# Loading a run's weight addresses into TensorE's registers one half-step earlier, from padded rows, in a macaron block of two mixture-of-experts layers and an RWKV attention

## What is computed

```python
x = x + 0.5 * ffn(ln(x))          # mixture of experts, top 2 of 8
x = x + attention(ln(x))          # RWKV: token shift, k, v, r, wkv recurrence over 512 tokens, Wo
x = x + 0.5 * ffn(ln(x))          # the same experts again

def ffn(x):
    probs = softmax(x @ gate_w)                       # (8*512, 8)
    weights, indices = top_k(probs, 2); weights /= weights.sum(-1)
    for i in range(8):                                # w1, w3: 128x512, w2: 512x128
        wi = where(indices == i, weights, 0).sum(-1)
        out += ((silu(x @ w1[i]) * (x @ w3[i])) @ w2[i]) * wi
```

## Time and profile before

| | us |
|---|---|
| median of 3 executions | 621.75 |
| lowest, highest | 621.48, 623.04 |
| the profiled execution | 623.24 |
| its span, first to last instruction | 621.4 |
| PE busy with matmuls | 521.1 (84% of the span) |
| PE weight loads busy | 477.7 (77%) |
| DVE busy | 423.8 (68%) |
| POOL busy | 389.3 (63%) |
| ACT busy | 318.9 (51%) |
| mean granted TensorE clock | 0.97 |

### The profile page before, as it was taken

How to read it: one execution, slowest core, us unless ns; L and a number is a source line. 1 busy time by engine, 2 the same in 40 slices (tenths; PEclk the granted TensorE clock), 3 DMA queues, 4 the chain that set the end, 5 groups by cost and what they waited for, 6 DMA issues and landing times.

```text
span 621.4 us, 18551 instructions
## 1 busy us (share of the span) xinstructions
PE 521.1 (84%) x5866; PEld 477.7 (77%) x5866; DVE 423.8 (68%) x1218; ACT 318.9 (51%) x703; POOL 389.3 (63%) x490
## 2 busy tenths in 40 slices
PE   1235899999999899998999959998989999989930
PEld 1233789898978789877898849887879899978930
DVE  4862863556878988799998955887788765215431
ACT  5433674444585565756676534776473444434410
POOL 1171058489999970599808996003949887835973
PEclk9999899999999999999999979999998999989985
DMA  8963233544232221212221133111121442313332
GB/s 284 329 192 113 61 92 114 156 137 124 79 116 65 78 74 53 74 60 73 78 66 53 59 101 87 49 37 36 54 81 57 121 112 83 103 45 99 91 89 59
DMA packets 89062, 59.55 MB, mean 96 GB/s; under 512 B 10256, under 2 KB 82704, under 8 KB 88976
## 3 DMA queue, kind: packets, MB, share of 16 engines
q1 hardware_dynamic: 55296, 29.97, 16.5%
q0 software_dynamic: 8192, 16.79, 8.9%
q10 hardware_dynamic: 25488, 11.61, 6.5%
HBM read 28.65 MB, written 29.69 MB: 94 GB/s over the span
## 4 chain that ended last, share of the span: by engine, by line
PE 56%; DVE 13%; ACT 11%; issue 8%; POOL 8%; DMA 3%; POOLq 0%; ACTq 0%; DVEq 0%; SPq 0%
PE py L1259 18%; PE pa L1245 14%; PE pb L1245 12%; POOL rows_in L725 3%; ACT xn L817 3%; POOL yg L737 3%; DVE h L1114 3%; PE pT L1232 2%; PE bkB L1318 2%; PE bkB L1297 2%; ACT sil L798 2%; POOL pace L754 2%; PE bkA L1312 2%; ACT rT L778 1%; PE bkA L1297 1%
## 5 line engine op out<-in xcount | busy, mean ns | idle before, releaser
L725 POOL DMA_INDIRECT rows_in<-parts,slot x128 | 135.0, 1054 | 183.1 <-DVE slot L1039 161.2
L1114 DVE TENSOR_TENSOR h<-sil,pb 128x512 f32<-128x512 f32 x177 | 120.7, 686 | 127.3 <-ACT sil L798 79.6
L1259 PE MATMUL py<-ffn_w,h 128*128 x1416 | 198.6, 284 | 9.4 <-ACT yrow L783 9.0
L1259 PEld LDWEIGHTS py<-ffn_w,h 128*128 128x128 f32 x1416 | 175.2, 195 | 15.2 <-issue 12.3
L1245 PE MATMUL pa<-rT,ffn_w 128*128 128x128 f16 (+1 forms) x1752 | 151.7, 233 | 22.8 <-issue 12.5
L1245 PE MATMUL pb<-rT,ffn_w 128*128 128x128 f16 (+1 forms) x1752 | 154.5, 232 | 0.0
L1245 PEld LDWEIGHTS pa<-rT,ffn_w 128*128 x1752 | 124.2, 99 | 37.6 <-issue 26.4
L737 POOL DMA_INDIRECT yg<-rows_out,slot x128 | 125.4, 980 | 38.6 <-issue 22.8
L754 POOL MEMSET pace<- 128x544 uint8 x223 | 127.7, 573 | 0.1
L1245 PEld LDWEIGHTS pb<-rT,ffn_w 128*128 x1752 | 122.2, 98 | 6.8
L798 ACT ACTIVATE sil<-pa 128x512 f32<-128x512 f32 x177 | 105.3, 595 | 40.4 <-PE pa L1245 39.9
(11 more groups left out here) (156 smaller groups left out, 459.2 us busy)
## 6 DMA issues: line engine op xcount, KB each, us to landing
rows_out<-yrow ACTq DMA_DIRECT2D x177, 64.0 KB, 1.9
rin<-rows_in SPq DMA_DIRECT2D x65, 128.0 KB
rows_in<-zrow SPq DMA_DIRECT2D x34, 128.0 KB, 2.0
shared<-in_w SPq DMA_DIRECT2D x16, 256.0 KB, 6.7
rin<-rows_in SPq DMA_DIRECT2D x47, 64.0 KB
rows_in<-zrow SPq DMA_DIRECT2D x2, 1472.0 KB, 11.0
xres<-in_x SPq DMA_DIRECT2D x4, 512.0 KB, 6.3
ffn_w<-in_w SPq DMA_DIRECT2D x8, 256.0 KB, 5.2
```

Source lines behind the costliest of these rows:

```text
L725: pool.indirect_dma_start(rows_in[g][:], bass.IndirectOffsetOnAxis(ap=slot[:, c, at:at + 1], axis=0), parts[:, at, :], None).then_inc(s_sc ...
L1114: dve.tensor_tensor(h[:, t % RING, :], sil[:, t % 2, :], pb[t % 2][:], ALU.mult).then_inc(s_h, 1)
L1259: mm = pe.matmul(py[:], h[:, step % RING, at:at + T], w, start=(c == 0), stop=(c == FC - 1))
```

## The change

```diff
@@ -146,7 +146,8 @@
 TILE_OF = [tile_of(t) for t in range(TILES)]
 NE = tuple(STEPS[r] if OPEN[r] or MORE[r] else NQ[r] for r in range(RUNS))
-ESTART = tuple(sum(NE[:r]) for r in range(RUNS + 1))
+LINE = 16
+ESTART = tuple(sum(-(-n // LINE) * LINE for n in NE[:r]) for r in range(RUNS + 1))
@@ -1049,7 +1050,7 @@
                 np, n = PAIRS[run], NE[run]
-                te, ids = teid[:, 0:n], eid[:, ESTART[run]:ESTART[run + 1]]
+                te, ids = teid[:, 0:n], eid[:, ESTART[run]:ESTART[run] + n]
@@ -1265,7 +1266,7 @@
                 _, found = nc.values_load_multi_w_load_instructions(
-                    eid[0:1, ESTART[run]:ESTART[run + 1]], engines=(mybir.EngineType.PE,), min_val=0,
+                    eid[0:1, ESTART[run]:ESTART[run] + NE[run]], engines=(mybir.EngineType.PE,), min_val=0,
@@ -1273,8 +1274,8 @@
             def tile(t):
                 q, half, _ = TILE_OF[t]
-                if t in START:
-                    load_experts(run_of(t))
+                if t == 0:
+                    load_experts(0)
                 if half == 0:
                     pe.wait_ge(s_rT, q + 1)
                 wait(pe, s_h, t - 1)
@@ -1282,6 +1283,8 @@
                 if t + 1 < TILES and TILE_OF[t + 1][1] == 0:
                     turn_tile(TILE_OF[t + 1][0])
                 up(t, pb[t % 2], 2).then_inc(s_up3, 1)
+                if t + 1 in START[:RUNS]:
+                    load_experts(run_of(t + 1))
                 if t >= SKEW:
                     down(t - SKEW)
```

## The result

| | before | changed |
|---|---|---|
| median, us | 622.06 (4 runs, 621.48 to 623.04) | 614.77 (4 runs, 614.15 to 615.39) |
| profiled execution, us | 623.24 | 615.32 |
| its span, us | 621.4 | 613.5 |

The ratio is 0.9882, 95% interval 0.9864 to 0.9899: 7.3 us less, 8.5 to 6.3 by the interval. The forecast was 612.0 us with a range of 609.0 to 617.8. Of the two kernels one execution each was profiled; these two differ by 7.9 us, and that is what the sum of the prediction (-9.8) has to be held against.

A forecast was written before the change was run, and what follows sets the result against it. PE, busy 84% of the span, was taken to bound the kernel. Pauses -7.2, step 131 -0.3 more, clock -0.6 at step 101 and -1.7 at 162 sum to -9.8: 621.75 to 612.0 us, range 609.0 to 617.8.

The forecast's parts named there:

- part 1: Padding shortens the `eid` loads at steps 101, 131 and 162 from 7.10, 2.20, 2.87 to 2.37, 0.995, 1.13 us.
- Rival (a): Loads of `eid` keep their lengths, set by count or traffic, not place: about +0.6, 622.4 us; chance 0.06.
- part 2: Loads move in front of `down`; each new pause is load + 0.15 - lead; pauses sum to -7.2 us.
- Run 1: Steps 23 to 45, load of 16 words: PE's pause grows from 0.58 to 0.92 us, +0.3.
- run 5: Steps 101 to 130, load of 30 words: pause falls from 6.81 to 2.4 us, -4.4; smaller clock fall, -0.6.
- run 7: Steps 140 to 161, load of 22 words, aligned before: pause goes from 1.38 to 1.6 us, +0.2.
- run 8: Step 162 to the end, load of 12 words: pause falls from 2.58 to 1.2 us, -1.4; clock stays up, -1.7.
- Runs 2 and 4: Loads for steps 46 and 92: -0.1 us, beside a copy wait; 0, delay taken up by a later rows wait.
- part 3: Granted clock stays up behind steps 131 and 162 (-1.7 us at 162), falls less at step 101 (-0.6).
- The cap at run 6: `h` of step 131 on DVE limits the gain: of 1.9 + 1.55 us at most 2.4, taken as -2.2.
- (c): Loads shorten, but the clock still falls as before at steps 101, 131 and 162: 614.6 us; chance 0.2.
- (b): Loads keep their lengths and the clock also falls at step 140, costing 1.7 us: 624.1 us; chance 0.03.

The follow-up runs named there:

- that with other places: Changed kernel with the runs' words in `eid` beginning 16, 32 or 48 bytes off a multiple of 64: 629.06 us in one execution.
- padding alone: Kernel before with the runs' words padded to multiples of 16 words, loads at their old place: 625.70 us, ratio 0.9860; on another chip 611.53 us, 0.9844.
- that with two loads moved: Against the kernel before: padding, with only the loads for steps 46 and 92 moved in front of `down`: 613.27 us, ratio 0.9880.

## Why the prediction held, and which of its steps failed

**The lengths of the loads** (part 1): right, by the two groups of the earlier trace rows, and shown from both sides by the runs. The largest unknown, 30 aligned words, was 2.44 us against 2.37. The Trainium skill gives about 200 ns per register even in bulk ("Runtime: NRT & Kernel Launch", "Instruction fetch mechanics"); the section has the runtime's own register loads in view, these are the kernel's, from SBUF. The figure comes near only for words that begin off a multiple of 16 bytes (237 to 267 ns each); the others cost 70 to 113 ns a word. Rival (a) is out.

**The pauses at runs 1, 5, 7, 8** (part 2): right in kind and nearly in size. Behind the end of a load `down` follows by 0.15 us as assumed. I measure from the start of `pb` to the start of `down` and take off what the same step has where no load stands between them (0.67 us, 0.85 at step 100). Run 1 loses 0.89 us (0.92 forecast), run 5 2.50 (2.4), run 7 1.57 (1.6), run 8 1.04 (1.2). Run 3 loses 0.55 where 0.9 was forecast: its load, which took 1.51 us before, took 1.11 instead of the 1.3 that was put in. The size at run 7 holds for this trace alone; in the three traces of the move on the first chip of the experiments its pause is 1.85 to 1.87 us instead of 1.41. In the total run 7 added -0.13 us where +0.2 was forecast.

**Runs 2 and 4** failed. For run 2 I had put -0.1, "the load runs while `down(42)` waits for the copy anyway": it cost 0.55. The load did not start 0.6 us ahead of the last matmul of `pb`, but with it (182.39 against 182.37): shortly before, PE and its sequencer had both stood in a wait for a copy, and behind such a wait there is no lead. `down` then had to wait for the end of the load at 183.51, half a microsecond behind the end of the copy at 182.98. The trace of before could not show the lead there, since the sequencer's next instruction was itself waiting. For run 4 I had counted on a later wait for rows to take up the delay; the delay was 0.36 us, and the rows came 0.48 later too, though POOL sent the last scatter at the same time (354.86 against 354.84). Runs 1 to 4 together: +0.3 forecast, +0.96 measured, hidden in the total by the 0.95 us that the clock gave at the start. That is luck: without it the two profiles would differ by 6.9 us, and the sum of -9.8 would be 2.9 off instead of 1.9.

**The clock** (part 3): right at run 8 (-3.15 us for pause and clock, -3.1 forecast) and at run 6, where it stays up. Wrong at run 5, "a fall there, of run 8's size: -0.6". In this profile the clock is down for 6.2 us of work where it was 4.6 before, so the term was about +0.8. It isn't a constant of the kernel. Behind pauses of 1.9 to 2.5 us at this step it fell for 6.8 us in one profile of the changed kernel, for 3.4 in the other, in that with other places and in one of padding alone, and not at all in the other profile of padding alone and in that with two loads moved. A size of fall should have been given as a range there, 0 to 3 us. At run 5 as a whole -5.0 was forecast and -3.1 measured: -4.3 for the pause as forecast, +0.5 for the rows, +0.8 for the clock.

**The cap at run 6** held: `h` of step 131 follows the attention's work on DVE without idle time again (467.59), 3.06 us earlier than before, which is just what PE was ahead at step 130. The part settled at -1.5 instead of -2.2.

**The rivals.** The time is that of (c), 614.6 us, but not by its mechanism: of its three falls of the clock one was left. (b) was not met: run 7's pause was 1.41 us and the clock stayed. The move by itself, which the prediction had as +0.6 us in rival (a) (its terms add up to +0.4), was measured: 1.7 us slower.

## What to carry to other kernels

When a value or an address is loaded into an engine's registers in the middle of the work, look at the length of each such load, and let the words begin at a multiple of 16 bytes (tried here on TensorE alone): that rounding was worth 1.5% of a kernel whose diff spoke of something else. What lies ahead of such a load on its engine covers it, what lies behind does not; so put it behind long instructions that need few of the sequencer's own (a projection), or into a wait that exists anyway, and split it if it is longer than its cover. A change that does two things is judged only when each half has been run.

## What the hardware showed unexpectedly

- A load of registers has two prices: about 0.24 us per word and up to 0.25 us for all of them, if its first word is off a multiple of 16 bytes (9 words 2.2 to 2.4 us, 12 words 2.9 to 3.0, 16 words 4.0, 22 words 5.3, 30 words 7.1 to 7.3; places 4, 8 and 12 bytes off were seen); else 0.9 to 1.0 us for 9, 0.9 to 1.0 for 12, 1.1 to 1.8 for 16, 1.9 to 2.0 for 22 and 2.4 to 2.5 for 30. The short loads cross multiples of 64 bytes without being longer (30 words from 32 bytes behind one: 2.39 us).
- The granted clock fell or stayed up behind nearly the same pause at the same step, from one execution to the next: behind 1.95 to 1.96 us in front of step 6, and behind 1.9 to 2.5 us at run 5. During or behind every pause of 2.8 us or more at the start of a run it fell.
- Chips differ by more than the change is worth: 621.3, 630.4 and 635.1 us for the kernel before. On the slowest one the changed kernel took 8.6 us more behind step 176 alone. Ratios to the kernel before on the same chip were steady, at 0.988 and 0.990 for the changed kernel.
